# Attention in units of four head pairs, value product written transposed in eight places of the array, and xs_lo computed on GpSimd

## The reference

```python
x = attn_layer(shift_tokens(x), Wqkv[i], q_scale[i], k_scale[i], Wo[i]) + x
x = ffn_layer(shift_tokens(x), ln_g[i], ln_b[i], W1[i], b1[i], W2[i], b2[i]) + x
# attn_layer, 16 heads of 64, windows of 32 rows that see the window before too:
q, k, v = split(x @ Wqkv);  q, k = rotary(l2norm(q) * qs), rotary(l2norm(k) * ksc)
sim  = einsum('bhwie,bhwje->bhwij', bq, bk2) * 8.0      # 32 queries against 64 keys
attn = softmax(where(mask, -max, sim), -1)
out  = einsum('bhwij,bhwje->bhwie', attn, bv2) @ Wo
```

## Time and profile before

| | |
|---|---|
| median of 3 runs | 3748.63 us (3744.89 to 3750.44) |
| profiled execution | 3743.95 us, of it span 3742.1 us |
| TensorE clock granted | 0.976 on the mean |

### The profile page before, as it was taken

How to read it: one execution, slowest core, us unless ns; L and a number is a source line. 1 busy time by engine, 2 the same in 40 slices (tenths; PEclk the granted TensorE clock), 3 DMA queues, 4 the chain that set the end, 5 groups by cost and what they waited for, 6 DMA issues and landing times.

```text
span 3742.1 us, 161812 instructions
## 1 busy us (share of the span) xinstructions
PE 3470.4 (93%) x63907; PEld 2773.6 (74%) x63907; DVE 3141.4 (84%) x6016; ACT 2271.7 (61%) x4159; POOL 1852.4 (50%) x1604
## 2 busy tenths in 40 slices
PE   5758999999999999999999999999999999999996
PEld 2326787877788878788878788877788887788784
DVE  8987888888788888788888788888788888888883
ACT  2014666666666666666666666666566666666663
POOL 2435455454554554545554445545455445455541
PEclk9988999999999999999999999999999999999998
DMA  2002423323333323333223333232432332332332
GB/s 84 9 28 50 104 60 70 77 54 78 91 67 77 72 56 80 82 77 77 64 64 76 85 77 71 57 77 67 95 72 59 73 77 54 79 74 60 70 77 73
DMA packets 186363, 261.00 MB, mean 70 GB/s; under 512 B 31670, under 2 KB 89908, under 8 KB 185396
## 3 DMA queue, kind: packets, MB, share of 16 engines
q1 hardware_dynamic: 186164, 258.24, 30.7%
HBM read 22.30 MB, written 4.19 MB: 7 GB/s over the span
## 4 chain that ended last, share of the span: by engine, by line
PE 71%; issue 13%; DVE 7%; POOL 3%; ACT 3%; SPq 2%; DMA 1%; ACTq 0%; POOLq 0%; DVEq 0%
PE bank L653 9%; PE bank L705 8%; PE bank L637 7%; PE bank L613 6%; PE obank L687 6%; PE bank L738 5%; PE bank L615 4%; PE bank L614 4%; PE bank L697 4%; PE bank L663 4%; PE bank L745 3%; DVE xs_lo L1139 3%; PE bank L647 2%; PE bank L628 2%; PE bank L630 2%
## 5 line engine op out<-in xcount | busy, mean ns | idle before, releaser
L951 POOL TENSOR_TENSOR qn<-qn,rinv 128x512 f32<-128x512 f32 x768 | 805.4, 1065 | 1382.1 <-DVE rinv L1198 1382.1
L945 POOL TENSOR_TENSOR qn<-ropec,ropes 128x512 f32<-128x512 f32 x768 | 982.9, 1294 | 274.6 <-DVE ropes L1150 230.8
L1149 DVE TENSOR_TENSOR ropec<-bank,rots 128x512 f32<-128x512 f32 x768 | 526.7, 686 | 116.0 <-ACT sq L833 63.7
L1158 DVE TENSOR_REDUCE ss<-sq 128x8 f32<-128x512 f32 x768 | 513.2, 679 | 88.0 <-ACT sq L833 82.6
L1150 DVE TENSOR_TENSOR ropes<-bank,rots 128x512 f32<-128x512 f32 x768 | 523.7, 682 | 0.0
L833 ACT ACTIVATE sq<-bank 128x512 f32<-128x512 f32 x768 | 448.8, 598 | 87.7 <-PE bank L615 68.9
L855 ACT ACTIVATE Pr<-Pr 128x512 f32<-128x512 f32 x384 | 241.9, 630 | 399.1 <-DVE Pr L1209 396.9
L637 PE MATMUL bank<-ident,qn 128*128 128x128 f32 x3072 | 464.1, 274 | 18.4 <-POOL qn L951 14.9
L653 PEld LDWEIGHTS bank<-kT,qT 64*32 64x32 f32 x24576 | 363.1, 107 | 122.0 <-issue 121.9
L613 PE MATMUL bank<-wqkv_hi,xs_hi 128*128 128x512 f32 x768 | 353.1, 460 | 99.2 <-DVE xs_lo L1139 90.8
L637 PEld LDWEIGHTS bank<-ident,qn 128*128 128x128 f32 x3072 | 375.9, 141 | 83.9 <-issue 18.8
(11 more groups left out here) (137 smaller groups left out, 6215.9 us busy)
## 6 DMA issues: line engine op xcount, KB each, us to landing
V<-Vt SPq DMA_DIRECT2D x576, 260.0 KB
V<-Vt SPq DMA_DIRECT2D x192, 130.0 KB
V<-Vt SPq DMA_DIRECT2D x192, 65.0 KB
xres<-X SPq DMA_DIRECT2D x96, 128.0 KB
X<-x SPq DMA_DIRECT2D x96, 128.0 KB, 2.0
wqkv_raw<-L_ffn_Wqkv SPq DMA_DIRECT2D x6, 1536.0 KB
xraw<-X SPq DMA_DIRECT2D x97, 64.0 KB
xraw<-X SPq DMA_DIRECT2D x97, 63.8 KB
```

The lines of the kernel that those rows point to most:

```text
L945: pool.tensor_tensor(qn[:, c, :], ropec[:, c % ROPE_RING, :], ropes[:, c % ROPE_RING, :], ALU.add).then_inc(rope_sum.sem, 1)
L951: pool.tensor_tensor(heads8(qn[:, c, :]), heads8(qn[:, c, :]), rinv[:, 8 * c:8 * c + 8].unsqueeze(2).broadcast_to([P, 8, DH]), ALU.mult).t ...
L1149: dve.tensor_tensor(halves(ropec[:, c % ROPE_RING, :]), raw, table(t, 2 * kind), ALU.mult)
L1158: dve.tensor_reduce(ss[:, 8 * c:8 * c + 8], heads8(sq[:, c % 2, :]), AX.X, ALU.add).then_inc(ss_done.sem, 1)
```

## The change

A unit is now one row tile and four pairs of heads, both parities, where it was eight heads of one parity.

1. qk (`b_qk`): a unit's 32 matmuls alternate between the two row halves of the array and rotate over the four strips, eight places in all; each half writes its own bank. The mask is two matmuls of 256 columns.
2. The softmax is divided by its sum before the product: VectorE sums exp's result (`b_rs`) and takes the reciprocal, GpSimd multiplies (`b_pn`). V loses its column of ones.
3. pv (`b_pv`): V is the weights and PT streams, 64 matmuls of 32 columns in a unit for 32 of 65, and the result is already transposed. The ot transposes and the On multiply are gone; ScalarE copies from PSUM to OT.
4. qk and pv share two banks (`pair`): each waits until the step before it in `PAIR_ORDER` has been read out. The projections get a third bank.
5. V is placed tile by tile, 8 and 10 DMAs, each of half the size.
6. xs_lo is computed on GpSimd.
7. `ORDER` is rewritten for all four engines.

```diff
 ORDER["pe"]
-        qk.0' wo.0'' qk.1' proj.7 v.0 mean.0'' pt.0' qk.2' var.0'' pt.1' pv.0' qk.3' v.1 v.2 ln.0'' v.3
+        w2.0''' tr.5' pv.2'' tr.6' pt.3'' proj.6 tr.7' pv.3'' proj.7 qk.0' wo.0'' qk.1' v.0 pt.0' mean.0''
+        qk.2' v.1 var.0'' v.2 v.3 pv.0' pt.1' ln.0'' qk.3' tr.0 w1.0''
@@ banks
-        b_proj, b_trA, b_trB, b_sim, b_c = bank[0:2], bank[2], bank[3], bank[4], bank[5]
+        pair = ps("pair", [P, 2, 512])
+        b_proj, b_trA, b_trB, b_c = [bank[0], bank[1], bank[4]], bank[2], bank[3], bank[5]
+        b_sim = pair[:, :, 0:4 * 2 * WIN]
+        b_o = pair[:, :, 4 * 2 * WIN:512]
@@ place_v(n, t)
+                hold(sp, sp_held, v_copied.sem, v_copied.at(n, 2 * t + 2))
+                hold(sp, sp_held, o_full.sem, o_full.at(n - 1, 2 * t + 2))
@@ b_qk, tensor
+                pair_free("qk", b, u)
+                for par in range(2):
+                    pe.matmul(b_sim[:, par, :], identb[:], maskb[:, 1 if t else 0, :].unsqueeze(1).broadcast_to([P, 4, 2 * WIN]),
+                              start=True, stop=False, skip_group_check=True)
+                for j in range(4):
                     for w in range(4):
+                        for par in range(2):
+                            rows = slice(64 * par, 64 * par + 64)
+                            q0 = t * P + w * WIN
+                            mm = pe.matmul(b_sim[w * WIN:(w + 1) * WIN, par, j * 2 * WIN:(j + 1) * 2 * WIN],
+                                           qT[rows, 4 * mh + j, q0:q0 + WIN],
+                                           kT[rows, 4 * mh + j, q0:q0 + 2 * WIN],
...
@@ b_pv
-                for j in range(4):
-                    for w in range(4):
-                        for slot in range(2):
-                            rows = slice(64 * slot, 64 * slot + 64)
-                            wg = 4 * t + w
-                            mm = pe.matmul(obank[w * WIN:(w + 1) * WIN, slot, j * 65:j * 65 + 65],
-                                           PT[rows, u % 2, j * P + w * WIN:j * P + (w + 1) * WIN],
-                                           V[rows, wg // 2, wg % 2, j, par, :],
+                pair_free("pv", b, u)
+                for w in range(4):
+                    for jj in range(2):
+                        wg = 4 * t + w
+                        for odd in range(2):
+                            j = 2 * jj + odd
+                            for dh in range(2):
+                                for par in range(2):
+                                    rows = slice(64 * par, 64 * par + 64)
+                                    strip = 32 * (2 * (par ^ odd) + dh)
+                                    mm = pe.matmul(b_o[strip:strip + 32, odd, jj * P + w * WIN:jj * P + (w + 1) * WIN],
+                                                   V[rows, wg // 2, wg % 2, 4 * mh + j, 32 * dh:32 * dh + 32],
+                                                   PT[rows, u % 2, j * P + w * WIN:j * P + (w + 1) * WIN],
...
@@ gpsimd
+            def b_pn(b, u):
+                pool.wait_ge(rs_done.sem, rs_done.at(b, u + 1))
+                pool.tensor_tensor(heads8(Pr[:, u % 2, :]), heads8(Pr[:, u % 2, :]),
+                                   rs[:, u % 2, :].unsqueeze(2).broadcast_to([P, 8, 2 * WIN]), ALU.mult).then_inc(p_scaled.sem, 1)
+            def a_xs(a, _):
+                pool.wait_ge(xs_hi_done.sem, xs_hi_done.at(a, 1))
+                pool.tensor_tensor(xs_lo[:], xraw[:], xs_hi[:].bitcast(F32), ALU.subtract).then_inc(xs_lo_done.sem, 1)
@@ vector
-            def b_pv(b, u):
...
+            def b_rs(b, u):
+                dve.wait_ge(p_ready.sem, p_ready.at(b, u + 1))
+                dve.tensor_reduce(rsum[:, u % 2, :], heads8(Pr[:, u % 2, :]), AX.X, ALU.add).then_inc(rsum_done.sem, 1)
+                dve.wait_ge(rsum_done.sem, rsum_done.at(b, u + 1))
+                dve.reciprocal(rs[:, u % 2, :], rsum[:, u % 2, :]).then_inc(rs_done.sem, 1)
```

More of the change, by code:

```diff
@@ L246, in build @@
         v_copied = per_batch("v_copied", 4)
-        v_placed = per_batch("v_placed", 16 * V_DMAS)
+        v_placed = [per_batch(f"v_placed_{t}", 16 * V_DMAS[t]) for t in range(2)]
         trA_full = per_batch("trA_full", 8)
@@ L446, in load_x, with place_v, move @@
                 sp.dma_start(xraw[64:P, 1:T], X[64:P, bass.ds(g * T, T - 1)]).then_inc(x_loaded.sem, 16)
[L448 to L468, removed]
+            def place_v(n, t):
+                hold(sp, sp_held, v_copied.sem, v_copied.at(n, 2 * t + 2))
+                hold(sp, sp_held, o_full.sem, o_full.at(n - 1, 2 * t + 2))
+                for par in range(2):
+                    half = 64 * par
+                    def move(dst, w, odd, src, rows, tile=t):
+                        d = V[dst:dst + rows, 2 * t + w, odd].rearrange("p m c -> p (m c)")
+                        v = Vt[src:src + rows, tile, par].rearrange("p m c -> p (m c)")
+                        sp.dma_start(d, v).then_inc(v_placed[t].sem, 16)
+                    move(half, 0, 1, 0, 64)
+                    move(half, 1, 1, 64, 64)
+                    move(half, 1, 0, WIN, 64)
+                    move(half + WIN, 0, 0, 0, WIN)
+                    if t == 1:
+                        move(half, 0, 0, P - WIN, WIN, tile=0)
             def body(n, g, lags, layer, c_layers, conv_c=None):
@@ L533, in _ @@
             for m in range(3):
-                mm = pe.transpose(b_sim[:, m * P:(m + 1) * P], la_w_rows[:, m, :], ident[:])
+                mm = pe.transpose(bank[4][:, m * P:(m + 1) * P], la_w_rows[:, m, :], ident[:])
             mm.then_inc(la_wt, 1)
@@ L587, in la_channels @@
                         pe.wait_ge(la_yc.sem, la_yc.at(i - 1, 1))
-                    pe.matmul(obank[:, 0, :], gather[:, m, :], Pr[:, m % 2, :], start=m == 0, stop=m == LH - 1).then_inc(la_ym.sem, 1)
+                    pe.matmul(pair[:, 0, :], gather[:, m, :], Pr[:, m % 2, :], start=m == 0, stop=m == LH - 1).then_inc(la_ym.sem, 1)
             def la_output(i):
@@ L593, in la_output @@
                 for t in range(4):
-                    mm = pe.matmul(obank[:, 1, t * P:(t + 1) * P], la_y[:, t * P:(t + 1) * P], la_w[:, 3, :], start=True, stop=True)
+                    mm = pe.matmul(pair[:, 1, t * P:(t + 1) * P], la_y[:, t * P:(t + 1) * P], la_w[:, 3, :], start=True, stop=True)
                 mm.then_inc(la_po.sem, 1)
@@ L1122, in la_residual @@
                 rows = X1[:, bass.ds((i - 1) * 4, 4), :]
-                dve.tensor_tensor(rows, rows, obank[:, 1, :].rearrange("p (t c) -> p t c", c=D), ALU.add).then_inc(la_out.sem, 1)
+                dve.tensor_tensor(rows, rows, pair[:, 1, :].rearrange("p (t c) -> p t c", c=D), ALU.add).then_inc(la_out.sem, 1)
             la_pipeline(dve, la_head, la_channels)
@@ L1134, in _ @@
             dve.memset(ss[:], 1.0).then_inc(setup, 1)
-            def a_xs(a, _):
-                dve.wait_ge(xs_hi_done.sem, xs_hi_done.at(a, 1))
-                dve.tensor_tensor(xs_lo[:], xraw[:], xs_hi[:].bitcast(F32), ALU.subtract).then_inc(xs_lo_done.sem, 1)
             def a_proj(a, c, layer):
```

162 lines of the change are left out of this document (72 added, 90 removed).

## The result

| | before | after |
|---|---|---|
| median of 4 runs | 3748.8 us (3744.9 to 3750.4) | 4529.4 us (4523.5 to 4534.3) |
| profiled execution, its span | 3743.95, 3742.1 us | 4527.8, 4526.0 us |
| TensorE clock granted, mean | 0.976 | 0.928 |

The changed kernel is slower: 1.208 times the time before, with an interval of 1.206 to 1.210. The forecast was 3645 us, in a range of 3550 to 3790; none of the four rivals comes near either.

The account below looks back on a forecast made before the run. It took TensorE's steps in a body, plus its waits at a few joints, as the bound. The terms summed to -1.07 us a body, times 96 -103 us: 3645 us, in a range of 3550 to 3790.

Parts of the forecast that it names:

- pv doubles its instructions: Value product on TensorE: 64 more instruction pairs a unit cost 0.55 us, +2.20 us a body (from 0.76 to 4.4).
- The ot transposes: Four ot steps of 0.43 us on TensorE go, as the value product comes out transposed: -1.74 us a body.
- qk: qk's load bursts on TensorE take pv's pattern with both row halves: 0.244 us a unit, -0.98 us a body.
- The mask: Two mask matmuls of 256 columns for one of 512, with one more weight load: +0.1 us for four.
- rival A: The second half of pv is cheap, small matmuls at half the present time: -2.0 us a body, 3555 us; chance 0.17.
- Rival C: pv's row halves clash in one PSUM bank, 13.3 ns a pair: +1.17 us a body, 3856 us; chance 0.11.
- The signs that the prediction named: TensorE's pv step 1.3 to 1.4 us, above 1.8 C, below 1.05 A; wrong if pairs cost other than 8 to 10 ns.
- The wait for xs_lo: TensorE's first projection no longer waits, with xs_lo on GpSimd and the body's end recut: -0.95 us a body.
- New waits: Thin margins at joints between engines, shared qk and pv banks included, break here and there: +0.3 us a body (0 to 1.3).
- Rivals B and D: B: sum and GpSimd chains arrive late, 3740 us, chance 0.15; D: ScalarE waits for V's DMAs, 3830 us, chance 0.09.
- p_scaled of unit 3: Unit 3's normalised softmax: sum, reciprocal and product end at 12.5 us into the body, before pt.3 is due at 13.1.

Follow-up runs that it names:

- four_places: The changed kernel with pv as 32 matmuls of 64 weight columns a unit in place of 64 of 32; 3657.5 us, 0.976 of before.
- eight_two_units: The changed kernel with 64 pv matmuls of 32 weight columns only in units 1 and 3, 32 of 64 in the rest; 3735.4 us.
- half_pv: The changed kernel computing only the first 32 of each head's 64 value columns, half of pv's matmuls; 3643.8 us.
- double_two_units: The kernel before with pv's matmuls issued twice in units 1 and 3; 3912.5 us.
- double_three_units: The kernel before with pv's matmuls issued twice in units 1, 2 and 3; 4402.1 us.

## Why the prediction was wrong

The failed step is the one on pv, "pv doubles its instructions": it priced the 64 added pairs of a unit by their own time and their code at nothing. No term stood for it, and the sum took for granted that TensorE always has its next instruction. That fetch costs 43.6 us less about 33.5, which is what the beats of four_places and eight_two_units lead to with two more units of 0.175: some 10 us in each of 60 ordinary bodies. That is 600 us, where the whole span grew by 784. What the profile of before held: q8 with 138 packets, none in a quiet body, beside 1386 instructions that the change made 1873. I never asked what happens to a loop that fits, once it grows by a third.

The Trainium skill, "Runtime: NRT & Kernel Launch", section Instruction fetch mechanics, puts TensorE's instruction memory at 2048 instructions, filled in blocks of 16 KiB, calls the crossing of a block "mostly hidden", and says that a taken branch whose target isn't in the current window of two pages forces a fetch. This case's traces bear out the block (16,384 bytes). That the crossing is hidden holds at 5.3 packets a body and not at 7 to 8. The window of two pages doesn't fit: bodies of 1386 and of 1642 instructions, more than five blocks long, jump back without one packet. The step comes somewhere between 1642 and 1745, below 2048.

The other terms, read in quiet bodies of before, four_places and eight_two_units, as sums of TensorE's steps from start to start:

- The ot transposes: 1.75 us a body before, gone. Forecast -1.74.
- qk: 4.17 to 3.17 us a body, -1.00. Forecast -0.98. The mask: 1.26 to 1.24, forecast +0.10.
- pv: 0.80 us a unit before, 1.07 with 32 matmuls in four places, 1.23 with 64 in eight. So +0.43 a unit in place of +0.55; the forecast of 1.3 to 1.4 for the step was a little high, and rival A's bound of 1.05 was not reached. Rival C is refuted: 128 pairs in 1.22 us are 9.5 ns a pair, where the clash's price was 13.3, although both row halves write one bank. The signs that the prediction named would have misled here: the pv step of the changed kernel is 1.9 us on the mean, above the 1.8 that was to mean C, but only with the pauses in it, and the pairs' own pace lies within the 8 to 10 ns outside of which the forecast was to be wrong. No sign stood for the fetch.
- The wait for xs_lo: 4.7 us for 7 bodies in the quiet stretch of before, 0.67 a body, and none in that of four_places. Forecast -0.95, which was a mean with the turns in it (90.8 us over 96 bodies). xs_lo took 0.73 us on GpSimd (forecast 0.5 to 0.7).
- New waits: none. Four_places' quiet window has no idle time of 0.1 us or more that another engine released, and its TensorE is idle for 1 us in 320. In place of the +0.3 us stand dearer neighbours: the same tr transposes take 3.97 us a body for 3.51, the v projections 3.19 for 2.97, ln 0.55 for 0.36. Why, I didn't test; they now stand behind other steps. That is +0.9 us. Rivals B and D are refuted: no such waits, for GpSimd's product or for V; in the whole run of the changed kernel ScalarE's Vt copy waited 7.9 us for V's DMAs. And rival A could have gained 0.8 us a body at most: half_pv, with a pv step of 0.69 us, stands at 32.75 us against the 33.5 below.

In sum a body without the fetch would take about 33.5 us; the forecast's beat was 33.26. That they come so close is in part luck, since pv and the mask came 0.6 us below the forecast, and the xs_lo wait and the neighbours 0.9 above it. Two figures of the prediction were slips without effect: p_scaled of unit 3 ends at 12.2 by its own terms and not at 12.5, and rival C decides from about 11 ns a pair on and not from 11.8. The net of these terms, -0.8 us, is a tenth of what was left out. And they'd not have carried the time to 3645: at the layers' turns, which I left alone, two units of eight places already add 56 us over four_places.

## What to carry to other kernels

Count the instructions in the loop body of each engine before and after, and look at the instruction queue's packets in a quiet body: here the loop that fetched nothing had a limit somewhere above it, and a change that added small instructions crossed it all at once. A wait that nothing releases, inside a burst of identical matmuls, was the sign of it. Where the same work can be done with fewer, wider matmuls, that is the version to run: here it took the change from 21% slower to 2.4% faster.

## What the runs showed of the hardware

- In the first five layers TensorE's loop of 1642 instructions ran without a fetch, one of 1745 fetched 9 packets of 16,384 bytes in every body; more than its own size (1745 x 63 bytes are 6.7 packets).
- Near the limit the place of the loop matters: in the last layer of double_two_units, with the same 1642 instructions, every other body fetched 9 packets and took 40.5 to 41.9 us against 36.4 to 36.9. double_three_units did the same there (41.2 to 42.8 against 37.3 to 37.6) with 1770 instructions, of which it had fetched 9 packets in every body before. So no single number of instructions is the limit, and what the place does to it wasn't tested.
- After a pause of 2.5 us at the body's end TensorE came back at its 1.2 GHz level (granted clock 0.50), so a stall is paid for a second time: 0.43 for 0.23 us a matmul over the next three projections.
- In the changed kernel nine in ten of TensorE's pauses of 0.5 us or more that nothing released ended 1.2 to 1.8 us after an instruction packet had ended.
- 64 pairs of pv take 0.69 us with 32 weight columns (half_pv) and 1.07 with 64 (four_places), both in four places; 128 pairs with 32 columns take 1.23 (eight_two_units).
